# Gram matrices by small matmuls: laps of two tiles worked on by halves, a ring of eleven input tiles, later stores

## The reference

```python
r_inputs = jax.random.normal(key, (2048, 64, 256), jnp.float32)

def reference(inputs):
    Z = jnp.einsum('bnd,bmd->bnm', inputs, inputs)
    li, lj = jnp.tril_indices(64, k=-1)
    return Z[:, li, lj]                      # 2048 x 2016
```

## Time and profile before

| | before |
|---|---|
| median of 3 runs | 403.62 us (401.89 to 403.79) |
| the profiled execution | 403.43 us |
| its span | 401.6 us |
| PE busy | 365.2 us (91%) |
| DVE busy | 362.3 us (90%) |
| ACT busy | 178.4 us (44%) |
| POOL busy | 197.7 us (49%) |
| read from HBM / written | 134.22 MB / 16.52 MB, 375 GB/s over the span |
| granted TensorE clock, mean | 0.989 |

### The profile page before, as it was taken

One profiled execution on the slowest core, in us unless ns is written; L12 is line 12 of the kernel. 1 busy time (PEld: TensorE's weight loads), 2 busy tenths in 40 slices (PEclk: granted clock), 3 DMA queues, 4 the chain that ended last, 5 costly groups with the idle time before them and its releaser, 6 DMA issues.

```text
span 401.6 us, 68674 instructions
## 1 busy us (share of the span) xinstructions
PE 365.2 (91%) x33024; PEld 359.8 (90%) x33024; DVE 362.3 (90%) x240; ACT 178.4 (44%) x821; POOL 197.7 (49%) x974
## 2 busy tenths in 40 slices
PE   4439999999999999999999999998999899998960
PEld 4439999999999999999999999998989899998960
DVE  3417899999999999999999998989999798998995
ACT  0011224555445544465445654453554344455463
POOL 1000047282833866086817475283835738184585
PEclk9999999999999999999999999999999999999995
DMA  8299999999999999999999999999999999998417
GB/s 319 105 351 427 420 422 423 420 405 421 422 425 402 422 425 421 422 415 425 420 424 413 421 417 419 352 399 417 381 425 360 425 370 422 403 366 339 138 31 206
DMA packets 21274, 151.01 MB, mean 376 GB/s; under 512 B 2688, under 2 KB 2816, under 8 KB 4864
## 3 DMA queue, kind: packets, MB, share of 16 engines
q1 hardware_dynamic: 18752, 135.77, 83.8%
q10 hardware_dynamic: 2496, 14.97, 9.6%
HBM read 134.22 MB, written 16.52 MB: 375 GB/s over the span
## 4 chain that ended last, share of the span: by engine, by line
DVE 43%; DMA 34%; issue 13%; PE 8%; DVEq 0%
DVE x_turned L233 38%; DMA x_in<-x_dram 34%; PE bank_set L311 8%; DVE row_halves L250 3%; DVE x_in L257 1%; DVE packed_rows L153 1%; DVE packed_rows L142 0%; DVE x_turned L262 0%; DVEq L249 0%; DVEq L232 0%; DVEq L74 0%; DVEq L282 0%
## 5 line engine op out<-in xcount | busy, mean ns | idle before, releaser
L311 PE MATMUL bank_set<-x_turned 32*64 32x64 f32 x33024 | 365.2, 237 | 23.3 <-issue 15.1
L311 PEld LDWEIGHTS bank_set<-x_turned 32*64 32x64 f32 x33024 | 359.8, 132 | 28.5 <-issue 16.1
L233 DVE STREAM_TRANSPOSE x_turned<-x_in 128x2048 f32<-128x2048 f32 x128 | 287.9, 2280 | 33.8 <-PE bank_set L311 18.4
L153 POOL COPY packed_rows<-row_halves 32x32 f32<-32x32 f32 (+30 forms) x930 | 190.0, 204 | 198.3 <-DVE row_halves L250 98.6
L342 ACT COPY products<-bank_set 128x512 f32<-128x512 f32 (+1 forms) x91 | 68.4, 758 | 153.1 <-PE bank_set L311 141.0
L250 DVE STREAM_TRANSPOSE row_halves<-products 128x1024 f32<-128x1024 f32 x60 | 72.2, 1205 | 0.0
L142 ACT COPY packed_rows<-row_halves 128x32 f32<-128x32 f32 (+30 forms) x465 | 61.4, 220 | 16.6 <-DVE row_halves L250 16.5
L148 ACT COPY packed_rows<-row_halves 128x128 f32<-128x128 f32 x240 | 54.0, 299 | 27.8 <-DMA y_dram<-packed_rows 16.1
L342 ACT ACT_TABLE_LOAD x1 | 1.3, 1283 | 19.6 <-PE bank_set L311 19.6
L153 POOL COPY packed_rows<-x_in 32x32 f32<-32x32 f32 (+30 forms) x31 | 4.9, 209 | 0.1
L257 DVE STREAM_TRANSPOSE x_in<-products 128x512 f32<-128x512 f32 (+1 forms) x5 | 4.8, 998 | 0.0
## 6 DMA issues: line engine op xcount, KB each, us to landing
x_in<-x_dram SPq DMA_DIRECT2D x128, 1024.0 KB, 16.2
y_dram<-packed_rows ACTq DMA_DIRECT2D x22, 504.0 KB, 9.2
y_dram<-packed_rows ACTq DMA_DIRECT2D x6, 252.0 KB
y_dram<-packed_rows ACTq DMA_DIRECT2D x24, 63.0 KB
y_dram<-packed_rows SPq DMA_DIRECT2D x2, 504.0 KB, 4.7
y_dram<-packed_rows SPq DMA_DIRECT2D x1, 380.0 KB
y_dram<-packed_rows ACTq DMA_DIRECT2D x1, 380.0 KB
y_dram<-packed_rows SPq DMA_DIRECT2D x1, 124.0 KB
```

The lines of the kernel that those rows point to most:

```text
L153: return copy(packed_rows[first:first + BLOCK, group % 2, :, at + BLOCK:at + i], halves(group)[first + BLOCK:first + HALF, i, :, 0:i - BLOCK])
L233: nc.vector.transpose(x_turned[:, j].rearrange("p c b s (h u n v) -> p u v (c b s h) n", h=ROWS // BLOCK, u=PAIRS, v=PAIR), x_in[:, k]).th ...
L311: done = nc.tensor.matmul(bank_sets[s][side * HALF:(side + 1) * HALF, g, at, :].rearrange("r (n u v) -> r u n v", u=PAIRS, v=PAIR), rows, ...
```

## The change

It goes through the whole kernel, with one idea in each part:

- A lap is two tiles (`LAP = 2`), which divides 128, so the tile of zeros and its fills go. `x_turned` has two places instead of three, and each PSUM set takes one tile.
- A tile is worked on by halves (`PARTIALS` = 2): DVE turns chunks 0 to 3 and chunks 4 to 7 with an instruction each, and PE multiplies one half when it is there. `turned` and `multiplied` (before `tile_multiplied`) are semaphores for each half. ACT keeps one tile at a time.
- The ring of input tiles is 11 long, and the hold on loads 4 and 5 is gone. `products` has two places for groups instead of three; the pieces lag 10 tiles instead of 11.
- The stores of groups 13 and 14 are both issued by SP behind its last load (`LATE_STORES` = 13).

```diff
-    IN_RING = 8
-    LATE = 4
-    LAP = 3
-    LAPS = -(-TILES // LAP)
-    BLANK = LAPS * LAP - TILES
-    SET_TILES = (2, 1)
-    SETS = len(SET_TILES)
+    IN_RING = 11
+    LAP = 2
+    LAPS = TILES // LAP
+    SETS = LAP
+    PARTIALS = 2
+    PARTIAL = CHUNKS // PARTIALS
...
-    KEPT_RING = 3
+    KEPT_RING = 2
...
-    PIECE_LAG = GROUP_TILES + 3
-    PACK_LAG = 2 * PIECE_LAG - 3
+    PIECE_LAG = GROUP_TILES + 2
+    PACK_LAG = 2 * PIECE_LAG - 2
...
+    LATE_STORES = GROUPS - 3
...
                 if t >= IN_RING:
                     lap, j = place(t - IN_RING)
-                    sync.wait_ge(turned[j], (lap + 1) * LAP)
-                elif t == LATE:
-                    lap, j = place(0)
-                    sync.wait_ge(tile_multiplied[j], lap + 1)
-                elif t == LATE + 1:
-                    lap, j = place(0)
-                    sync.wait_ge(kept[set_of(j)[0]], (lap + 2) * LAP)
+                    sync.wait_ge(turned[j][PARTIALS - 1], (lap + 1) * LAP)
...
-            sync.wait_ge(packed_home, (GROUPS - 1) * PIECES)
-            sync.wait_ge(packed_across, (GROUPS - 1) * LONG_PIECES)
-            store(sync, GROUPS - 2, slice(0, PACKED), WHOLE_SIDES)
+            for group in range(LATE_STORES, GROUPS - 1):
+                sync.wait_ge(packed_home, (group + 1) * PIECES)
+                sync.wait_ge(packed_across, (group + 1) * LONG_PIECES)
+                store(sync, group, slice(0, PACKED), WHOLE_SIDES)
...
                 dve.wait_ge(loaded[k], (t // IN_RING + 1) * 16)
-                if lap > 0:
-                    dve.wait_ge(tile_multiplied[j], lap)
-                nc.vector.transpose(
-                    x_turned[:, j].rearrange("p c b s (h u n v) -> p u v (c b s h) n", h=ROWS // BLOCK, u=PAIRS, v=PAIR),
-                    x_in[:, k]).then_inc(turned[j], LAP)
+                for h in range(PARTIALS):
+                    chunks = slice(h * PARTIAL, (h + 1) * PARTIAL)
+                    if lap > 0:
+                        dve.wait_ge(multiplied[j][h], lap)
+                    nc.vector.transpose(
+                        x_turned[:, j, chunks].rearrange(
+                            "p c b s (h u n v) -> p u v (c b s h) n", h=ROWS // BLOCK, u=PAIRS, v=PAIR),
+                        x_in[:, k].rearrange("p (r d) -> p r d", r=JOINED)[
+                            :, :, chunks.start * BLOCK:chunks.stop * BLOCK]).then_inc(turned[j][h], LAP)
...
+                for h in range(PARTIALS):
+                    pe.wait_ge(turned[j][h], count)
+                    for slot in range(SLOTS):
+                        last_slot = h == PARTIALS - 1 and slot == SLOTS - 1
+                        if j == LAP - 1 and last_slot:
+                            pe.reg_add(count, count, LAP)
+                        for c in range(h * PARTIAL, (h + 1) * PARTIAL):
+                            if last_slot and c == CHUNKS - 2:
+                                pe.wait_ge(kept[1 - j], count)
...
+                    done.then_inc(multiplied[j][h], 1)
...
+            for t in range(TILES):
+                keep(t)
+                if stores < LATE_STORES and n >= (stores + 1) * PIECES * 4:
+                    store_whole(stores)
...
+                while n + PACK_LAG < 2 * (t + 1):
+                    pack(n)
+                    n += 1
```

More of the change, by code:

```diff
@@ L113, in place, with wait_kept @@
         def place(t):
-            return divmod(t + BLANK, LAP)
-        def set_of(j):
-            return (0, j) if j < SET_TILES[0] else (1, j - SET_TILES[0])
+            return divmod(t, LAP)
+        def wait_kept(engine, t):
+            lap, s = place(t)
+            engine.wait_ge(kept[s], (lap + 2) * LAP)
         def piece_rows(piece):
@@ L240, in turn_rows @@
                 if piece == 0:
-                    lap, j = place((group + 1) * GROUP_TILES - 1)
-                    s = set_of(j)[0]
-                    dve.wait_ge(kept[s], (lap + 2) * LAP)
+                    wait_kept(dve, (group + 1) * GROUP_TILES - 1)
                 if group > 0:
@@ L272, in _ @@
             for run in range(RUNS):
[L273 to L275 removed]
+                wait_kept(dve, (GROUPS - 1) * GROUP_TILES + (run + 1) * GROUP_TILES // RUNS - 1)
                 if run < RUNS - 1:
@@ L295, in multiply @@
             def multiply(j):
[L297 to L316, removed]
@@ L318, in multiply @@
-                done.then_inc(tile_multiplied[j], 1)
+                for h in range(PARTIALS):
[7 more added lines that the diff above has]
+                                pe.wait_ge(kept[1 - j], count)
+                            for g in range(QUADRANTS):
+                                for side in range(SIDES):
+                                    rows = x_turned[g * BLOCK:(g + 1) * BLOCK, j, c, slot, side]
+                                    done = nc.tensor.matmul(
+                                        bank_sets[j][side * HALF:(side + 1) * HALF, g, slot, :].rearrange(
+                                            "r (n u v) -> r u n v", u=PAIRS, v=PAIR),
+                                        rows,
+                                        rows.rearrange("d (h u e) -> d u h e", h=ROWS // BLOCK, u=PAIRS),
+                                        start=c == 0 and slot == 0, stop=c == CHUNKS - 1 and slot == SLOTS - 1)
+                    done.then_inc(multiplied[j][h], 1)
@@ L329, in _, with keep @@
         def _(act):
[L330 to L348, removed]
+            def keep(t):
+                lap, s = place(t)
+                group, in_group = divmod(t, GROUP_TILES)
+                act.wait_ge(multiplied[s][PARTIALS - 1], lap + 1)
+                if group >= KEPT_RING and in_group == 0:
+                    act.wait_ge(rows_turned, (group - KEPT_RING + 1) * PIECES)
+                nc.scalar.copy(
+                    products[:, group % KEPT_RING, :, in_group * PER_SIDE:(in_group + 1) * PER_SIDE].rearrange(
+                        "p i (g b) -> p i g b", b=SLOTS),
+                    bank_sets[s][:, :, 0:SLOTS, :].rearrange("p g b i -> p i g b")).then_inc(kept[s], LAP)
             def pack(n):
@@ L374, in _ @@
             few = 0
[L375 to L388, removed]
+            for t in range(TILES):
+                keep(t)
+                if stores < LATE_STORES and n >= (stores + 1) * PIECES * 4:
+                    store_whole(stores)
+                    stores += 1
+                    few = len(FEW_LANES) if by_few(stores - 1) else 0
+                elif few > 0:
+                    store(act, stores - 1, slice(0, PACKED), FEW_LANES[-few:][:1])
+                    few -= 1
+                while n + PACK_LAG < 2 * (t + 1):
+                    pack(n)
+                    n += 1
             for n in range(n, LAST_HOME):
```

8 lines of the change are left out of this document (2 added, 6 removed).

## The result

The changed kernel took 398.27 us (median of 5 runs, 397.73 to 398.54) against 403.62 us (401.89 to 403.99) for the kernel before: a ratio of 0.9887, 95% interval 0.9865 to 0.991. The forecast was 400.0 us, in a range of 394 to 408, and "faster". The profiled execution took 398.30 us with a span of 396.5 us: 5.1 us less than that of before, where 3.4 had been added up.

The account below looks back on a forecast made before the run. The prediction saw a start bound by PE, a middle by DVE and a last third by DMA. Its terms +8.1 - 10.6 + 0.2 - 1.1 = -3.4 us took 403.43 to 400.0 us, range 394 to 408.

Parts of the forecast that it names:

- Turning by halves: DVE's turning from tile 12: two tiles and a piece take 5.65 us instead of 5.51, costing +8.1 us over 58 pairs.
- The rival of strided halves: DVE's half turns: every 20 ns more on a half costs 4.6 us, giving 404 to 407 us; chance 0.12.
- PE's pace: PE's laps of two tiles: 5.61 us a pair, 0.04 under DVE's 5.65, so PE is no bound.
- The rival of PE as the bound: PE's hand-over by halves: further waits could make a pair 5.81 us, +9.3, giving 409 us; chance 0.13.
- The ring of 11: DVE's waits for loads: three more tiles raise the lead from 14 to 22 us, so 10.6 us of waits go.
- The start: First lap: three pieces of PE's code, lap two at 29.0 us, tile 12 at 54.8 instead of 54.58: +0.2 us.
- Code behind eleven loads: First lap: if code waits for all loads queued, lap two begins near 45 us, giving 416 us; chance 0.04.
- code before PE asks: First lap: if code is fetched while PE first waits, lap two begins near 23 us, giving 394 us; chance 0.12.
- The end: Behind the last tile: with a lag of 10, one piece instead of two follows on DVE, -1.1 us.
- The rule on jumps: PE's jumps back: the skill's rule has far branches force a fetch, adding some 78 us, giving 478 us; chance 0.01.

Follow-up runs that it names:

- after_whole: The changed kernel with tiles turned and handed over whole (PARTIALS = 1), still two places and a ring of 11: 412.03 us, ratio 1.0243.
- before_ring11: The kernel before with a ring of 11 input tiles instead of 8 and two places of kept products instead of three: 400.72 us, ratio 0.9969.
- after_ring8: The changed kernel with a ring of 8 input tiles instead of 11, nothing else: 401.93 us, ratio 0.9992.
- after_hold: The changed kernel with the old hold back: load 4 waits until PE has multiplied tile 0, load 5 until it is kept: 396.45 us, ratio 0.9864.
- after_lag11: The changed kernel with the pieces of turned rows, and the packing, 11 tiles late instead of 10: 398.31 us, ratio 0.9902.
- after_hold4: The changed kernel with load 4 held until PE has multiplied the first half of tile 1: 400.41 us, ratio 0.9961.
- before_nohold: The kernel before without the hold on loads 4 and 5: 408.10 us, ratio 1.015.

## Why the prediction was right, and where not

**Direction and size.** Faster was forecast, by 3.4 us; 5.1 came. The mechanism that was named held in its main line: waits for loads gone, DVE as the bound to the end, at a slightly longer pair.

**Turning by halves, +8.1.** Right, and a little less: 1.127 us from start to start, 5.634 a pair where 5.65 was put, 58 x 0.124 = 7.2 us. The eight stretches of input cost nothing over one. The rival of strided halves falls.

**PE's pace.** Right: while DVE still waited for PE, its waits stood 5.60 us apart (37.18, 42.78 and 48.38 us), so that is PE's pace for a pair, and the sum had 5.61. From there on the pairs ran at DVE's 5.63, with no wait on PE after 48.38 us. The margin of 0.03 us a pair is as narrow as the prediction said. The rival of PE as the bound falls for the halves; after_whole shows it as it would have been, with whole tiles in two places.

**The ring of 11, -10.6.** The waits went, but the reason was half wrong, and this is the step that failed: "The ring of 11. ... The new one has three tiles more, 14 + 3 x 2.83 = 22 us." It took the lead for a matter of places. By the same count a kernel that turns whole tiles needs 0.225 x 110 = 25 us against those 22, and so before_ring11 should have waited for some 3 us; measured against a DVE that never waits, its last products came 8.9 us late (383.56 against 50.62 + 3.37 + 58 x 5.51 + 1.13 = 374.7, by the spacing of the earlier trace rows). The lead is made by DMA while DVE is still slow, in the first 50 us, and the hold had taken some 7 us of that. The text gave the missing hold its price in code and forgot its worth in lead. So the count of 22 was some 6 us too high with the hold, the missing hold gave about as much back, and it was luck that the term came out. Without the hold 8 places don't do (after_ring8); with a shorter hold 11 places nearly do (after_hold).

**The start, +0.2.** Lap two near 28.5 where 29.0 was put, tile 12 at 54.25 where 54.8 was: -0.3 in place of +0.2. The bounds of 5.9 to 7.4 us a piece held for all three: 6.1 for the first, counted from 8.6 us, then 6.75 and 6.58. Code behind eleven loads, and code before PE asks, both fall.

**The end, -1.1.** Wrong as a term of its own. The lag moves a piece from behind the last tile to ahead of it, and a DVE that is never idle does the same work up to the same point: after_lag11 begins the last products 0.25 us later, not 1.1, and what the lag is worth it is worth in the start. The 1.1 us belong to the lateness by loads, which was 11.7 and not 10.6: DVE alone would have begun the last products at 54.58 + 58 x 5.51 + 1.13 = 375.3, and began at 387.0. (The rows show 9.9 of the 11.7 as idle time in front of DVE.) The two mistakes cancel in the sum.

**What made 5.1 of 3.4.** 0.9 us by the shorter pair, 0.5 by the start, and 0.2 behind 382.11 us, where 14.4 us were left instead of 14.6.

**The rule on jumps.** The trace agrees with the rows, not with the rule: four instruction packets in 64 laps, and a lap of two tiles inside 5.63 us. The page's row of that queue (packets, MB, share):

```profile
q8 instruction: 4, 0.07, 0.1%
```

## What to carry to other kernels

When three resources are all at nine tenths, find which one sets the pace in each third of the run, and what stock the faster one lays up for later: a buffer is worth only what somebody has time to put into it, so its size and the moment at which its filling begins have to be changed together. A hold on early transfers that speeds the first code has its price at the far end of the run, and the best length is where the two meet (here 396.45 us with the old hold, against 398.27 without, a difference not clear of noise, and 400.41 with a longer one). Before counting a moved instruction as gain at the end, ask whether its engine was ever idle in between.

## What the runs showed that was not expected

One of the 16 DMA engines fell behind the others by so much that it alone set when the last loads landed: with whole stores it was some 16 us behind the rest. How the stores are cut over partitions changes this: four-lane pieces against none made 1.8% (before_ring11 and its variant), and eight-lane pieces for all groups cost 4.6% (ratios of 1.0415 against 0.9961 for after_hold4).

Code comes to PE in 3.5 to 3.7 us a piece when DMA is quiet and in 5.9 to 7.4 when loads run, and that doesn't grow with the loads that are queued: from piece to piece 6.2 to 6.9 with eleven out (the changed kernel, after_lag11 and after_whole), 6.0 to 6.8 with eight (after_ring8 and before_nohold).

In the first lap a burst of 127 or 128 matmuls took 2.25 us whatever clock was granted. In after_hold the granted clock was 0.50 (1.2 GHz) from 17.5 to 30 us, behind gaps of some 4 us in PE's work, and it was 1.00 (2.4 GHz) throughout in the changed kernel, which had gaps as long. The burst that starts at 17.92 us lies in the first of these rows; the second is the stretch with the start of lap two:

```profile
17.50:20.00 2.50, 2.08 (x127) 2.06 (x128) 1.15 (x1) 0.00 (x0) 0.00 (x0) 0.50 0.87 344
20.00:30.00 10.00, 5.67 (x382) 5.50 (x374) 3.36 (x4) 1.17 (x2) 0.00 (x0) 0.50 0.99 401
```

Lap two also began at one pace: from 26 to 28 us after_hold ran 158 matmuls in 2 us at 0.50, and from 30 to 32 us the changed kernel ran 159 at 1.00.
